# A graph network's last stage: PE transposes written as products, unread products beside them, and index-only numbers made one stage earlier

## The reference

```python
q, k, v = (einsum('ni,hid->nhd', x, W) + b for each)
e = edge_weight[:, None, None] * We[None]
alpha = einsum('ehd,ehd->eh', q[dst], k[src] + e) / sqrt(d)
ex = exp(alpha - segment_max(alpha, dst)[dst])
w = ex / max(segment_sum(ex, dst)[dst], 1e-16)
agg = segment_sum(w[:, :, None] * (v[src] + e), dst)
out = (agg + skip).reshape(n, 128) @ Wo + bo + x
out = (out - mean) * rsqrt(var + 1e-5) * gamma + beta
x = layernorm(x + out)
```

## Time and profile before

| | |
|---|---|
| median of 3 runs | 1664.46 us (1663.15 to 1665.85) |
| the profiled execution | 1661.83 us, its span 1660.1 us |
| mean granted PE clock | 0.785 |
| PE busy | 951.5 us (57%) |
| DVE busy | 1228.8 us (74%) |
| ACT busy | 744.5 us (45%) |
| POOL busy | 1033.6 us (62%) |
| attention | from 1060.4 us to about 1567 us of the span |
| tail | from 1570.6 us to the end |

### The profile page before, as it was taken

One profiled execution on the slowest core, in us unless ns is written; L12 is line 12 of the kernel. 1 busy time (PEld: TensorE's weight loads), 2 busy tenths in 40 slices (PEclk: granted clock), 3 DMA queues, 4 the chain that ended last, 5 costly groups with the idle time before them and its releaser, 6 DMA issues. The chain is left out here.

```text
span 1660.1 us, 25479 instructions
## 1 busy us (share of the span) xinstructions
PE 951.5 (57%) x6058; PEld 775.4 (47%) x6058; DVE 1228.8 (74%) x3576; ACT 744.5 (45%) x1613; POOL 1033.6 (62%) x1170
## 2 busy tenths in 40 slices
PE   4567676999999688999899996300000000000096
PEld 3344344788788588998898983100000000000064
DVE  7999995788777554595652116599989899899876
ACT  1577776789889155552566436300000000000034
POOL 4777777777777023355782522677777777777453
PEclk9798989999999999999899998655555555555555
DMA  6344445899965055564462632567777777777311
GB/s 186 122 147 135 144 147 166 265 300 297 320 196 142 1 209 189 184 204 148 142 235 100 241 111 79 174 206 230 227 219 219 223 229 222 219 221 217 127 46 36
DMA packets 108892, 300.02 MB, mean 181 GB/s; under 512 B 22561, under 2 KB 40053, under 8 KB 108636
## 3 DMA queue, kind: packets, MB, share of 16 engines
q1 hardware_dynamic: 49004, 139.91, 26.3%
q0 software_dynamic: 33440, 80.96, 16.8%
q10 hardware_dynamic: 26320, 77.63, 12.8%
HBM read 209.66 MB, written 88.76 MB: 180 GB/s over the span
## 5 line engine op out<-in xcount | busy, mean ns | idle before, releaser
L218 POOL DMA_INDIRECT fr_ring<-table,src_i x392 | 389.4, 993 | 140.2 <-issue 117.4
L1656 POOL DMA_INDIRECT e_kv<-kv_table,src_i x392 | 373.4, 953 | 119.7 <-issue 119.7
L1879 PE MATMUL n_ps<-ident,n_mm 128*8 128x128 f32 x1 | 0.4, 377 | 519.8 <-DVE n_mm L1984 519.8
L1879 PEld LDWEIGHTS n_ps<-ident,n_mm 128*8 128x8 f32 x1 | 0.1, 83 | 520.4 <-DVE n_mm L1984 520.4
L913 POOL CAST ly_af<-ly_au 128x640 fp32r<-128x640 uint16 x240 | 163.1, 725 | 128.4 <-DVE ly_part L1318 61.4
L594 PE MATMUL fe_ps<-fe_space 128*128 128x400 bf16 x591 | 150.5, 401 | 77.1 <-DVE fe_space L685 62.9
L685 DVE TENSOR_SCALAR fe_space<-fe_space,fr_key 128x400 bf16<-128x400 f16 x591 | 163.7, 344 | 3.6 <-PE fe_ps L594 3.3
L979 PE MATMUL ly_ps<-ly_af,ly_x_high 128*128 128x256 f32 (+1 forms) x650 | 159.8, 288 | 2.4 <-POOL ly_af L913 2.4
L1678 ACT ACTIVATE e_ps_m<-e_dif 128x56 f32<-128x56 f32 x56 | 12.4, 221 | 326.3 <-DVE e_dif L1768 326.3
L979 PE MATMUL ly_ps<-ly_af,ly_x_low 128*128 128x256 f32 (+1 forms) x650 | 156.3, 283 | 0.0
L594 PEld LDWEIGHTS fe_ps<-fe_space 128*128 128x128 bf16 x591 | 86.2, 146 | 141.4 <-issue 110.8
(11 more groups left out here) (406 smaller groups left out, 2642.1 us busy)
## 6 DMA issues: line engine op xcount, KB each, us to landing
ly_au<-edge_counts SPq DMA_DIRECT2D x88, 800.0 KB, 4.5
sums_att<-e_row ACTq DMA_DIRECT2D x56, 532.0 KB, 5.6
q_starts<-fe_space SPq DMA_DIRECT2D x56, 476.0 KB
e_qs<-q_starts SPq DMA_DIRECT2D x56, 476.0 KB, 4.4
fe_edge<-in_edgesT ACTq DMA_DIRECT2D x98, 256.0 KB, 3.8
edge_counts<-fe_space ACTq DMA_DIRECT2D x25, 800.0 KB, 3.8
fr_ring<-table,src_i POOLq DMA_INDIRECT x392
e_kv<-kv_table,src_i POOLq DMA_INDIRECT x392, 3.7
```

The lines of the kernel that those rows point to most:

```text
L218: pool.indirect_dma_start(f.ring[:, n % RB, t, 0:D], None, tab[0][:, :], bass.IndirectOffsetOnAxis(ap=src_i[:, at:at + 1].bitcast(U32), ax ...
L1656: pool.indirect_dma_start(kv[n % KS][:, t, :], None, kv_table[:, :], bass.IndirectOffsetOnAxis(ap=src_i[:, at:at + 1].bitcast(U32), axis=0 ...
```

## The change

Three edits, all around the tail.

1. `turn` writes its four transposes per pair as plain products with the identity (`matmul` in place of `transpose`), with the same operands.
2. A helper `busy(times, width, into)` issues products of the identity with weights, into PSUM that nobody reads before it is written anew. It is called three times in the preparation (2 of 512 columns, 1 of 256, 1 of 384) and, as the section `filler`, with 2 of 256 columns in each pair between `join` and `product`.
3. The numbers that depend on indices alone are made in the attention, on DVE after block 8 (`joints`), and held over the end of the stage; the iota that one of them needs stands at the head of POOL's attention queue. A small stage function `attention` calls both parts and the same barrier between them.

```diff
+        def attention():
+            with ExitStack() as st:
+                def held(name, shape):
+                    return st.enter_context(nc.sbuf_tensor(f"join_{name}", shape, F32))
+
+                j = Joints()
+                j.twice, j.lastf, j.key, j.brk = held("twice", [P, 1]), held("lastf", [P, 1]), held("key", [P, NT]), held("brk", [H, P + 1])
+                edges_attention(j)
+                end_stage()
+                tail_nodes(j)
...
+                        sp.wait_ge(keyed, 11)
...
+                        pool.iota(base[:, :], [[P, NT]], base=0, channel_multiplier=0,
+                                  allow_small_or_imprecise_dtypes=True).then_inc(based, 1)
...
+                        def joints():
+
+                            dve.wait_ge(lasts_in, 16)
+                            dve.wait_ge(based, 1)
+                            dve.tensor_tensor(same[:, :], bounds[:, 0:1], bounds[:, 1:2], ALU.is_equal).then_inc(keyed, 1)
+                            dve.tensor_tensor(j.twice[:, :], bounds[:, 2:3], bounds[:, 3:4], ALU.is_equal).then_inc(keyed, 1)
+                            dve.tensor_tensor(both[:, :], bounds[:, 0:1], bounds[:, 2:3], ALU.is_equal).then_inc(keyed, 1)
+                            dve.tensor_tensor(j.brk[:, :], last_of[:, 0:P + 1], last_of[:, 1:P + 2], ALU.not_equal).then_inc(keyed, 1)
+                            dve.tensor_copy(last_f[:, :], bounds[:, 0:1]).then_inc(keyed, 1)
+                            dve.wait_ge(keyed, 5)
+                            dve.tensor_tensor(both[:, :], both[:, :], j.twice[:, :], ALU.mult).then_inc(keyed, 1)
+                            dve.tensor_scalar(j.brk[:, :], j.brk[:, :], -BIG, None, ALU.mult).then_inc(keyed, 1)
+                            dve.scalar_tensor_tensor(key[:, :], last_f[:, :], 1.0, same[:, :], ALU.add, ALU.mult).then_inc(keyed, 1)
+                            dve.wait_ge(keyed, 8)
+                            dve.tensor_scalar(j.lastf[:, :], both[:, :], -1.0, 1.0, ALU.mult, ALU.add).then_inc(keyed, 1)
+                            dve.tensor_scalar(j.twice[:, :], same[:, :], 1.0, BIG, ALU.subtract, ALU.mult).then_inc(keyed, 1)
+                            dve.scalar_tensor_tensor(j.key[:, :], key[:, :].broadcast_to([P, NT]), -1.0, base[:, :], ALU.add, ALU.subtract).then_inc(keyed, 1)
+
...
                         for n in range(NB):
                             block_step(n)
+                            if n == 2 * QS:
+                                joints()
...
-                        pool.iota(base[:, :], [[P, NT]], base=0, channel_multiplier=0,
-                                  allow_small_or_imprecise_dtypes=True).then_inc(named, 1)
...
-                        pe.wait_ge(dv, 9)
+                        def busy(times, width, into):
+
+                            for _ in range(times):
+                                nc.tensor.matmul(into[:, 0:width], ident[:, :], wm[:, W_1:W_1 + width // D, :].rearrange("p a f -> p (a f)"), start=True, stop=True)
+
+                        busy(2, 4 * D, ps_o[0])
+                        pe.wait_ge(dv, 1)
                         nc.tensor.transpose(ps[0][0:H, 0:P], mm[:, :], ident[:, :]).then_inc(pe_s, 1)
-                        pe.wait_ge(dv, 11)
+                        busy(1, 2 * D, ps_o[0])
+                        pe.wait_ge(dv, 3)
                         nc.tensor.transpose(ps[1][:, 0:H], bs[:, :], ident[0:H, 0:H]).then_inc(pe_s, 1)
-                        pe.wait_ge(dv, 14)
+                        busy(1, 3 * D, ps_o[0])
+                        pe.wait_ge(dv, 6)
...
-                                nc.tensor.transpose(ps_t[g % 2][:, i * P:(i + 1) * P], agg[g % 2][:, i, :], ident[:, :])
-                                last = nc.tensor.transpose(ps_t[g % 2][0:H + 1, (2 + i) * P:(3 + i) * P], edge[g % 2][:, i, :], ident[:, :])
+                                nc.tensor.matmul(ps_t[g % 2][:, i * P:(i + 1) * P], agg[g % 2][:, i, :], ident[:, :], start=True, stop=True)
+                                last = nc.tensor.matmul(ps_t[g % 2][0:H + 1, (2 + i) * P:(3 + i) * P], edge[g % 2][:, i, :], ident[:, :], start=True, stop=True)
...
-                        in_steps(0, NG, [(2, turn), (0, join), (2, product)])
+                        def filler(g):
+                            busy(2, 2 * D, bank[7])
+
+                        in_steps(0, NG, [(2, turn), (0, join), (2, filler), (2, product)])
...
-                        after(dve.tensor_tensor(same[:, :], bounds[:, 0:1], bounds[:, 1:2], ALU.is_equal))
-                        after(dve.tensor_tensor(twice[:, :], bounds[:, 2:3], bounds[:, 3:4], ALU.is_equal))
...
-                        step(dve.scalar_tensor_tensor(key_rel[:, :], key[:, :].broadcast_to([P, NT]), -1.0, base[:, :], ALU.add, ALU.subtract))
                         for n in range(3):
                             hot(n)
                         dve.wait_ge(loaded, 16)
```

More of the change, by code:

```diff
@@ L77 @@
 class Front:
+    pass
+class Joints:
     pass
@@ L1593, in edges_attention @@
                 joined, breaking, spread, begun, tail_out, lasts_in = (sem(f"e4_{k}") for k in "joined breaking spread begun tail_out lasts_in".split())
-                head_known = sem("e4_head_known")
+                head_known, based, keyed = sem("e4_head_known"), sem("e4_based"), sem("e4_keyed")
+                same, both, last_f, key = (tensor(k, [P, 1]) for k in "same both last_f key".split())
+                base = tensor("base", [P, NT])
                 qs, kv, row = ring("qs", [P, TB, QW], QS), ring("kv", [P, TB, 2 * D], KS), ring("row", [P, CB, RW], RR)
@@ L1799, in tmp @@
                     return st.enter_context(nc.sbuf_tensor(f"n4_{name}", shape, dt))
-                loaded, named, dv, ks, pe_s, ac, masked, one_in = (sem(f"n4_{k}") for k in "loaded named dve key pe act masked one_in".split())
+                loaded, dv, pe_s, ac, masked, one_in = (sem(f"n4_{k}") for k in "loaded dve pe act masked one_in".split())
                 c = Counts(sem, "n4", "z zt raw num den inv agg tr at mm res stat var std rstd shift norm gain sum stat2 var2 std2 rstd2 shift2 norm2")
@@ L1805, in tail_nodes @@
                 head_row, head, scaled = tmp("head_row", [P, RW]), tmp("head", [P, H]), tmp("scaled", [P, RW])
-                last_f, key = tmp("last_f", [P, 1]), tmp("key", [P, 1])
-                base, key_rel = tmp("base", [P, NT]), tmp("key_rel", [P, NT])
-                same, twice, both, lastf = (tmp(k, [P, 1]) for k in "same twice both lastf".split())
                 mm, dif, sc = tmp("mm", [P, H]), tmp("dif", [P, 2, H]), tmp("sc", [P, 2, H])
-                brk, fs, bs = tmp("brk", [H, P + 1]), tmp("fs", [H, P]), tmp("bs", [H, P])
+                fs, bs = tmp("fs", [H, P]), tmp("bs", [H, P])
                 z, rows = tmp("z", [P, NT, P]), tmp("g", [P, NT, RW])
@@ L1953, in hot @@
                             if n < NT:
-                                dve.tensor_scalar(z[:, n, :], iota[:, :], key_rel[:, n:n + 1], None, ALU.is_equal).then_inc(c["z"], 1)
+                                dve.tensor_scalar(z[:, n, :], iota[:, :], j.key[:, n:n + 1], None, ALU.is_equal).then_inc(c["z"], 1)
                         for k in range(2):
@@ L1981, in _ @@
                         dve.wait_ge(loaded, 16)
-                        dve.tensor_tensor(head[:, :], head_row[:, MW:RW], twice[:, 0:1].broadcast_to([P, H]), ALU.add).then_inc(masked, 1)
+                        dve.tensor_tensor(head[:, :], head_row[:, MW:RW], j.twice[:, 0:1].broadcast_to([P, H]), ALU.add).then_inc(masked, 1)
                         dve.wait_ge(masked, 1)
@@ L1987, in _ @@
                         dve.wait_ge(pe_s, 1)
-                        after(dve.tensor_tensor_scan(fs[:, :], brk[:, 0:P], ps[0][0:H, 0:P], -BIG, ALU.add, ALU.max))
-                        after(dve.tensor_tensor_scan(bs[:, ::-1], brk[:, P:0:-1], fs[:, ::-1], -BIG, ALU.add, ALU.max))
+                        after(dve.tensor_tensor_scan(fs[:, :], j.brk[:, 0:P], ps[0][0:H, 0:P], -BIG, ALU.add, ALU.max))
+                        after(dve.tensor_tensor_scan(bs[:, ::-1], j.brk[:, P:0:-1], fs[:, ::-1], -BIG, ALU.add, ALU.max))
                         hot(5)
@@ L1999, in _ @@
                                           sc[:, 0, :].unsqueeze(1).broadcast_to([P, 2, H]), ALU.mult)
-                        after(dve.scalar_tensor_tensor(scaled[:, MW:RW], sc[:, 1, :], -1.0, lastf[:, 0:1].broadcast_to([P, H]), ALU.add, ALU.mult))
+                        after(dve.scalar_tensor_tensor(scaled[:, MW:RW], sc[:, 1, :], -1.0, j.lastf[:, 0:1].broadcast_to([P, H]), ALU.add, ALU.mult))
                         for n in range(7, ZA):
@@ L2080, in gnn_kernel @@
             middle,
-            edges_attention,
-            tail_nodes,
+            attention,
         ]
```

6 lines of the change are left out of this document (3 added, 3 removed).

## The result

The kernel after took 1668.9 us in the median of 8 runs (1663.9 to 1673.59), the kernel before 1663.17 in 8 runs beside it (1660.38 to 1665.85). The ratio is 1.0033, 95% interval [1.0019, 1.0047]: slower by 0.33%, about 5.5 us. The forecast was 1662.3 with 1665.8 as its upper end, and 0.07 for slower.

A forecast was written before the change was run, and what follows sets the result against it. PE at half clock was taken to bound the early tail, then DVE and ACT. Terms -3.05 + 0.6 + 0.3 = -2.15 from the median 1664.46 gave 1662.3 us, range 1659.6 to 1665.8.

The forecast's parts named there:

- the sum of the pair step: PE's work per pair in the tail loop: 4.76 us before, 3.9 after at full clock, 7.3 at half.
- to gain 3.05: Early pairs at full clock: DVE's first shift(1) comes at 1594.0 instead of 1597.06, a gain of 3.05 us.
- 0.3 for falls: Early pairs: a late clock rise or a fall before turn(0) costs 0.6 to 1.4, at one chance in three 0.3.
- three at 0.2: Late pairs: three turns fall into half speed and lose 0.2 us each, 0.6 in all.
- Rival 1: Tail clock stays at half, PE's 7.3 us step sets the period: +22.6, 1687 us; chance 0.05.
- rival 2: Clock flickers more: seven late turns at 0.3 and one early fall at 1.0 use up the gain, 1664.5; chance 0.22.
- The rule against the change: Turn in the early pairs: products cost two instructions, transposes one; 0.85 more per pair at half clock, +3.4, 1667.9 us.
- The other rule: Tail clock: transposes don't engage the full clock as matmuls do, which would give the 1662.3 us.
- the index part at 0: Moving 11 small DVE instructions from tail to attention, hidden by DVE's gather waits: 0; +2.3 us with the cover gone.
- the products at 0.42: Pair loop on PE: each product takes 0.42 us at full clock instead of 0.72, 1.66 for four.
- the DVE and ACT period of 5.75: Late pairs: DVE and ACT set a period of 5.75 us with no PE piece, so PE gains 0 there.
- the end of PE's part near pair 4: Tail: faster PE work can be worth something only up to about 1597 us; then DVE and ACT set the pace.

The follow-up runs named there:

- e7: The kernel after with the turn's products in the order agg, agg, edge, edge; 1.0017 of before.
- e9: The kernel before with only the pair's products reordered to eT, eT, aT, aT; 0.9990 of before.
- e14: The kernel after, filler kept, with the turn ordered agg, agg, edge, edge and the products eT, eT, aT, aT; 1662.1 us, 0.9994 of before.
- e6: The kernel after with the filler doubled from pair 4 on; 1.0015 of before.
- e3: The kernel after with the turn's real transposes kept, filler and preparation products staying; 0.9974 of before.
- e4: The kernel before plus preparation products and the moved index-only numbers, with transposes and no filler; 0.9974 of before.
- e12: The kernel after with real transposes and without the preparation's products, filler kept; 1.0011 of before.
- e2: The kernel after without the filler; 1.0087 of before.
- e1: The kernel before with only the index-only numbers moved into the attention; 1665.23 us beside 1665.54, 0.9995.
- e15: The same kernel as e4, measured again on one chip with e16; 0.9991 of before.
- e16: The same kernel as e10, measured again on one chip with e15; 0.9982 of before.
- e10: The kernel before with the preparation's products alone, index-only numbers left in the tail; 0.9992 of before.
- e11: The kernel before plus moved index-only numbers, preparation products, products ordered eT, eT, aT, aT and one unread 512-column product before the first turn; 0.9979 of before.

## Why the prediction was wrong, point by point

**The step that failed: the sum of the pair step, "after 3.9 at full clock, 7.3 at half".** Its terms and what the two chains above measured:

| | full, forecast | full, measured | half, forecast | half, measured |
|---|---|---|---|---|
| turn as products | 0.9 | 1.28 | 1.7 | 2.59 |
| joins | 0.5 | 0.71 | 1.01 | 1.31 |
| filler | 0.85 | 0.86 | 1.7 | 1.71 |
| products | 1.66 | 1.66 | 2.89 | 2.88 |
| step | 3.9 | 4.5 | 7.3 | 8.5 |

The turn was taken as eight instructions of 128 columns at their streaming time. It alternates between weights of 128 and of 9 columns (agg, edge), and the same surcharge that the forecast allowed the products, for their change between 9 and 128 rows, applies here. The size of it was in the earlier trace rows: 0.72 for two instructions of 0.21 each. The 0.21 of a transpose, in the same alternation, had hidden it: a transposed pair of agg and edge took no more than its streaming time. The joins behind the turn begin with the last such change, and are longer too; that this is their reason is read from the sizes and wasn't tested. For the turn and the products e7, e9 and e14 show the cause: reordered, the turn is 0.99 at full clock and the products 1.28.

**What it cost.** In the early pairs each full-clock step gained 0.24 over before instead of 0.86. In the first pairs one fall of 3.4 us (the step 0 to 1 took 5.96) and in pair 4 another (6.18). Without falls these pairs were to gain 3.05; measured at pair 4 is a loss of 1.5, so 4.5 are missing. Piece by piece: 2 x 0.6 for the two full steps, 2.1 for the fallen one against 3.9, 0.9 in pair 4 (6.18 against 5.3 before), 0.5 before move(0) (0.1 early instead of 0.6): together 4.7. So the length of the step is part of it and the two falls are the rest; the forecast had set aside 0.3 for falls here.

**"A turn that falls into half speed takes 0.9 longer, so ACT's copy is late by 0.7; three at 0.2."** For short falls in the late pairs this size was about right. A period with a fall of 3.4 us is longer, but the next one is shorter: 6.18 then 5.41 and 6.41 then 5.42 in e14, 6.59 then 5.47 and 6.41 then 5.41 in e7, against 5.75 each, so 0.1 to 0.6 a fall. Where PE still sets the pace one can cost more: 1.5 us in e6 (6.56 and 6.00, against 5.33 and 5.75 in before). What failed for the late pairs is that all falls were taken to be short. In a fall longer than a step PE sets the period with 8.5 us, by the mis-sized step: the two periods in the stretch of 13.6 us cost 3.4 together. Forecast for all late pairs was 0.6, measured 3.7.

**The rivals.** Rival 1 gave the mechanism ("it decides from a PE step over 5.75") and thought it through for a clock that never rises; rival 2 gave the flicker and priced a fall at 0.3. What came was rival 1's mechanism for rival 2's stretches. With the steps as measured, the two belong together, and a forecast that has a step of 7.3 against 5.75 needs a term for stretches of half clock longer than a step. e14, which has nearly the forecast's step, came to 1662.1 and 0.9994, within 0.1% of the forecast 0.9987 (1662.3 against 1664.46). Its interval holds that value and no gain at all as well, so it shows that the step's size carries the loss, not that the gain would have come.

**The clock.** That the preparation would be dense enough to raise it, was right: full from 7.2 us after the copy, which is 1574.4 on before's scale (forecast: "from about 1575"), and raw(0) 0.7 earlier (0.6). That it would be full for most of the tail was right in the sum: of the 82 us after the rise, some 58 were at full. It wasn't right in the length of the falls.

**The rule against the change.** The trace of before couldn't price the turn, and the Trainium skill, Perfetto Trace Analysis, section Transposes, that a logical transpose should use transpose, was given +3.4 and not followed. The runs bear it out: e3 against after is this edit alone, 0.9974 and 1.0033. What the trace shows of the cost at full clock is four instructions more, some 0.4 us, and as much again for the changes of shape. The other rule that was weighed against it, the Trainium skill, TensorE: Matmul & The Clock Gate, Part 4 (transposes don't engage the full clock as matmuls do), didn't decide anything in this loop: e4 kept full clock for 20.5 us from the preparation into a loop with transposes among products, e12 rose in one, and e2, with no transpose in the loop, stayed at half for 50 us. No run here has transposes alone.

**Right:** the index part at 0 (e1; e15 and e16), the products at 0.42, the filler's 0.86, the DVE and ACT period of 5.75 and the end of PE's part near pair 4 (e3, e4 and e14 all gain before it and nothing behind it). The forecast took PE at half clock in the earlier trace rows as not for lack of busy time, and that stands.

**Open:** what decides when the clock falls. In after it fell behind stretches with PE busy 4.08 of 5.00 us (1599.9 to 1604.9) and 1.53 of 2.50 (1619.5 to 1622), and stayed up through one with 4.03 of 5.00 (1612 to 1617); once down it stayed there for 13.6 us with PE busy all the time. One and the same kernel (e4 and e15) had it full for 20.5 and for 6.8 us. The spread of after's runs, 9.7 us, fits falls in different places, but only one execution of each was profiled. Open too is how much of the 0.3% lies in the 2.5 us ahead of the tail; the ratio over all runs and the tail's 5.2 us agree without them.

## What to carry to other kernels

Before work is added to an engine to raise its clock, compute its step at the low clock as well, and set it against the period of the others. Here 4.76 became 8.5 against 5.75, and one fall of 13.6 us cost 3.4. A step under that period is safe (e4); one slightly over it survived a fall of 10.2 us at a cost of 0.2 (e3). Take real transposes, and order small matmuls so that the shape of the weights changes once and not each time: both orders together were worth 0.7 us of the 4.5 us step of after. What paid in this kernel was work in a hole and not in the loop: products in the preparation alone (e4, e10, e15, e16) gave 0.08 to 0.26% in four measurements, of which two (e10, e15) don't exclude no gain. e11 beats the kernel before by 0.2% (1660.11 us, 0.9979), but isn't told apart from these.

## What was unexpected of the hardware

- Half the clock with TensorE busy 13.60 of 13.60 us, and 48.98 of 50 in e2, in plain f32 products of 128 to 256 columns.
- A change of the weights' shape between f32 products costs time beyond the streaming; that it is the weight load that then shows is likely but wasn't tested. The products of agg and edge alternating take 1.28 us for eight instructions at full clock, grouped 0.99; eT and aT alternating 1.66, grouped 1.28; at half clock 2.89 and 2.30. Transposes in the same alternation showed none of it: 0.21 each at half.
